# The end of the last block in two halves of two tiles, in a fused attention and LoRA-expert kernel

## The reference

```python
base1 = t @ w1.T
base3 = t @ w3.T
h1 = base1[None] + SCALING * jnp.einsum('etr,efr->etf', jnp.einsum('td,erd->etr', t, a1), b1)
h3 = base3[None] + SCALING * jnp.einsum('etr,efr->etf', jnp.einsum('td,erd->etr', t, a3), b3)
act = jax.nn.silu(h1) * h3
out_e = jnp.einsum('etf,df->etd', act, w2) + SCALING * jnp.einsum('etr,edr->etd', jnp.einsum('etf,erf->etr', act, a2), b2)
out = jnp.einsum('te,etd->td', weights, out_e)
```

## Time and profile before

| | |
|---|---|
| runs | 328.12, 328.14 and 328.87 us, median 328.14 us |
| profiled execution, its own time | 328.73 us |
| its span | 326.9 us (so 1.83 us lie outside the span) |
| mean granted TensorE clock | 0.979 |
| last matmul of `a2_product` ends | 317.50 us |
| last store issued | 324.54 us |

### The profile page before, as it was taken

How to read it: one execution, slowest core, us unless ns; L and a number is a source line. 1 busy time by engine, 2 the same in 40 slices (tenths; PEclk the granted TensorE clock), 3 DMA queues, 4 the chain that set the end, 5 groups by cost and what they waited for, 6 DMA issues and landing times.

```text
span 326.9 us, 4531 instructions
## 1 busy us (share of the span) xinstructions
PE 299.8 (92%) x1520; PEld 241.5 (74%) x1520; DVE 225.1 (69%) x608; ACT 193.9 (59%) x320; POOL 181.7 (56%) x164
## 2 busy tenths in 40 slices
PE   1875779999999999999999999999999999998992
PEld 1654557878888878878787888888787878886771
DVE  3568767697568956696668956795649845963373
ACT  1153566577674786587665777496646756854521
POOL 2111059935886278816794288718781389236910
PEclk9998789999999999999999999999999999999998
DMA  6512001000200002000200011000000000000000
GB/s 179 178 61 65 2 1 64 2 0 1 67 32 0 2 3 94 2 0 3 64 32 3 0 47 52 0 0 2 1 32 2 1 0 34 0 1 3 32 0 32
DMA packets 7127, 8.95 MB, mean 27 GB/s; under 512 B 1216, under 2 KB 3520, under 8 KB 7104
## 3 DMA queue, kind: packets, MB, share of 16 engines
q1 hardware_dynamic: 5520, 7.54, 7.0%
q10 hardware_dynamic: 1584, 1.12, 1.2%
HBM read 6.56 MB, written 2.10 MB: 26 GB/s over the span
## 4 chain that ended last, share of the span: by engine, by line
PE 72%; DVE 9%; issue 6%; POOL 6%; ACT 3%; DMA 2%; SPq 0%; DVEq 0%; POOLq 0%; ACTq 0%
PE h_ps L486 22%; PE h_ps L476 11%; PE z_ps L505 5%; PE b_ps L505 4%; PE odd_ps L519 4%; PE even_ps L344 4%; PE h_ps L456 3%; PE odd_ps L526 2%; PE b_ps L344 2%; PE even_ps L339 2%; PE z_ps L344 2%; PE odd_ps L389 2%; DMA wq_sb<-in_wq_dram 2%; POOL um_lo L1127 1%; PE z_ps L376 1%
## 5 line engine op out<-in xcount | busy, mean ns | idle before, releaser
L699 ACT ACTIVATE silu<-h_ps 128x512 f32<-128x512 f32 x64 | 38.1, 596 | 38.0 <-PE h_ps L486 37.1
L931 DVE TENSOR_TENSOR act_first<-silu,h_ps 128x512 f32<-128x512 f32 x32 | 22.0, 686 | 44.4 <-ACT silu L699 24.4
L486 PE MATMUL h_ps<-um_hi,b_hi 128*128 128x512 f32 x128 | 51.4, 401 | 0.1
L486 PE MATMUL h_ps<-um_hi,b_lo 128*128 128x512 f32 x128 | 50.9, 398 | 0.0
L486 PE MATMUL h_ps<-um_lo,b_hi 128*128 128x512 f32 x128 | 50.8, 397 | 0.0
L1121 POOL TENSOR_TENSOR heads<-e_o,rec_o 128x512 f32<-128x512 f32 x8 | 14.6, 1827 | 62.2 <-DVE rec_o L861 62.2
L1149 POOL TENSOR_TENSOR scaled<-act_second,ratio 128x512 f32<-128x512 f32 x24 | 30.9, 1287 | 21.0 <-DVE act_second L931 20.7
L476 PE MATMUL h_ps<-t_hi,w_hi 128*128 128x512 f32 x64 | 28.3, 442 | 1.9 <-ACT ratio L691 1.9
L1127 POOL TENSOR_TENSOR um_lo<-umf,um_hi 128x1024 fp32r<-128x1024 f32 x8 | 19.1, 2392 | 18.6 <-ACT um_hi L695 18.6
L931 DVE TENSOR_TENSOR act_second<-silu,h_ps 128x512 f32<-128x512 f32 x32 | 21.4, 683 | 10.7 <-PE h_ps L486 10.6
L486 PEld LDWEIGHTS h_ps<-um_lo,b_hi 128*128 128x128 f32 x128 | 24.2, 189 | 5.8
(11 more groups left out here) (161 smaller groups left out, 779.2 us busy)
## 6 DMA issues: line engine op xcount, KB each, us to landing
x_in<-in_x_dram SPq DMA_DIRECT2D x8, 256.0 KB, 3.0
out_dram<-y SPq DMA_DIRECT2D x8, 256.0 KB, 2.0
ctx_in<-in_ctx_t_dram SPq DMA_DIRECT2D x7, 256.0 KB, 3.2
w_raw<-in_w_t_dram SPq DMA_DIRECT2D x2, 256.0 KB, 6.3
b_raw<-in_b_dram ACTq DMA_DIRECT2D x2, 256.0 KB, 4.0
ctx_in<-in_ctx_t_dram ACTq DMA_DIRECT2D x1, 256.0 KB, 3.6
w2a_raw<-in_w_t_dram SPq DMA_DIRECT2D x1, 256.0 KB, 3.7
w2a_raw<-in_a_t_dram SPq DMA_DIRECT2D x1, 256.0 KB, 3.7
```

The costliest lines, as they stand in the source:

```text
L486: mm = nc.tensor.matmul(banks[n % 2][:], b13[w][:, s, cols], um[k][m][:, s, :], start=False, stop=(i == 2), skip_group_check=True)
L699: nc.scalar.activation(silu[:, n % SILU_RING, :], h1_ps[n % 2][:], ACT.Silu).then_inc(silu_done.sem, 1)
L931: nc.vector.tensor_tensor((act_first, act_second)[k][:, c, :], silu[:, n % SILU_RING, :], h3_ps[n % 2][:], ALU.mult).then_inc(act_done.sem, 1)
```

## The change

Only the last block is touched. On DVE the masks' products, the sum `v` and its low part are made in two halves of 256 tokens (two tiles), in the order products and sum of half 0, products and sum of half 1, then the two low parts. ACT makes the two high parts, and later the two copies to `o_t`. PE accumulates half 0 of the output in `odd_ps` and half 1 in `h1_ps[0]`, so that `w2_product` of the last block has six matmuls of 256 columns for a chunk in place of three of 512, and waits for two more semaphores at its first chunk, since `h1_ps[0]` must be free. The three matmuls of the second LoRA product are made for each half, then two transposes for each half, into `even_ps` and `h3_ps[0]`. DVE finishes two tiles and SP stores 128 KB, twice. What is computed stays the same.

```diff
+        last_out, last_turned = (odd_ps, h1_ps[0]), (even_ps, h3_ps[0])
...
-            store(BLOCKS - 1)
-            sp.wait_ge(stored.sem, stored.of(BLOCKS - 1))
+            for i in range(2):
+                sp.wait_ge(last_y, i + 1)
+                sp.dma_start(out[:, LAST * BLK + i * HALF:LAST * BLK + (i + 1) * HALF], flat(y)[:, half(i)])\
+                    .then_inc(last_stored, 16)
+            sp.wait_ge(stored.sem, stored.of(LAST - 1))
+            sp.wait_ge(last_stored, 32)
...
                         pe.wait_ge(o_t_done.sem, o_t_done.of(b - 1))
+                        pe.wait_ge(silu_done.sem, silu_done.of(b))
+                        pe.wait_ge(act_done.sem, act_done.of(b))
...
+                    for h in range(2):
+                        nc.tensor.matmul(last_out[h][:, 0:HALF], w2a2[w][:, c, 0:D], z_split[m][:, c, half(h)],
+                                         start=(c == 0 and i == 0), stop=False, skip_group_check=True)
...
-            b2_product(BLOCKS - 1)
-            tail(BLOCKS - 1)
+            for i in range(2):
+                pe.wait_ge(last_v_hi, i + 1)
+                pe.wait_ge(last_v_lo, i + 1)
+                for j, (w, m) in enumerate(TERMS):
+                    mm = nc.tensor.matmul(last_out[i][:, 0:HALF], b2_split[w][:], v_split[m][:, half(i)], start=False,
+                                          stop=(j == 2), skip_group_check=True)
+                mm.then_inc(last_o_t_mm, 1)
+            pe.wait_ge(y_done.sem, y_done.of(LAST - 1))
+            for i in range(2):
+                pe.wait_ge(last_o_t, i + 1)
+                for t in (2 * i, 2 * i + 1):
+                    mm = nc.tensor.transpose(last_turned[i][:, t * P:(t + 1) * P], o_t[:, t * P:(t + 1) * P], ident[:])
+                mm.then_inc(last_y_mm, 1)
...
-            v_high(BLOCKS - 1)
-            output_t(BLOCKS - 1)
+            for i in range(2):
+                sc.wait_ge(last_v, i + 1)
+                nc.scalar.copy(v_split[0][:, half(i)], v[:, half(i)]).then_inc(last_v_hi, 1)
+            for i in range(2):
+                sc.wait_ge(last_o_t_mm, i + 1)
+                nc.scalar.copy(o_t[:, half(i)], last_out[i][:, 0:HALF]).then_inc(last_o_t, 1)
...
-            v_sum(BLOCKS - 1)
-            v_low(BLOCKS - 1)
-            finish(BLOCKS - 1)
+            ve.wait_ge(a2z_mm.sem, a2z_mm.of(LAST))
+            ve.wait_ge(a2b_mm.sem, a2b_mm.of(LAST))
+            ve.wait_ge(mask_scaled.sem, mask_scaled.of(LAST))
+            ve.wait_ge(v_done.sem, v_done.of(LAST - 1))
+            for i in range(2):
+                for k in range(2):
+                    op = nc.vector.tensor_tensor(v_parts[:, k, half(i)], (z_ps, b_ps)[k][:, half(i)],
+                                                 masks[LAST % 2][:, k, half(i)], ALU.mult)
+                op.then_inc(last_v_part, 1)
+                ve.wait_ge(last_v_part, i + 1)
+                nc.vector.tensor_tensor(v[:, half(i)], v_parts[:, 0, half(i)], v_parts[:, 1, half(i)], ALU.add)\
+                    .then_inc(last_v, 1)
+            for i in range(2):
+                ve.wait_ge(last_v_hi, i + 1)
+                nc.vector.tensor_tensor(v_split[1][:, half(i)], v[:, half(i)], as_f32(v_split[0][:, half(i)]),
+                                        ALU.subtract).then_inc(last_v_lo, 1)
+            ve.wait_ge(w_first_done.sem, w_first_done.of(LAST))
+            ve.wait_ge(stored.sem, stored.of(LAST - 1))
+            for i in range(2):
+                ve.wait_ge(last_y_mm, i + 1)
+                for t in (2 * i, 2 * i + 1):
+                    op = nc.vector.scalar_tensor_tensor(out=y[:, t, :], in0=last_turned[i][:, t * P:(t + 1) * P],
+                                                        scalar=w_first[LAST % 2][:, t:t + 1],
+                                                        in1=x1[LAST % 3][:, t, :], op0=ALU.mult, op1=ALU.add)
+                op.then_inc(last_y, 1)
```

More of the change, by code:

```diff
@@ L275, in build_program @@
         stored = signal("stored", 16)
+        last_v_part = sem("last_v_part")
+        last_v = sem("last_v")
+        last_v_hi = sem("last_v_hi")
+        last_v_lo = sem("last_v_lo")
+        last_o_t_mm = sem("last_o_t_mm")
+        last_o_t = sem("last_o_t")
+        last_y_mm = sem("last_y_mm")
+        last_y = sem("last_y")
+        last_stored = sem("last_stored")
         def tile4(ap):
@@ L287, in build_program, with half @@
         PARTS = (slice(0, 2), slice(2, 3), slice(3, 4))
+        LAST = BLOCKS - 1
+        HALF = BLK // 2
+        def half(i):
+            return slice(i * HALF, (i + 1) * HALF)
         QKV_W_IN, ATTN_W_IN, LORA_W_IN, HIDDEN_W_IN, DOWN_W_IN = 4 * 16, 3 * 16, 5 * 16, 4 * 16, 3 * 16
@@ L517, in w2_product @@
                         pe.wait_ge(o_t_done.sem, o_t_done.of(b - 1))
+                        pe.wait_ge(silu_done.sem, silu_done.of(b))
+                        pe.wait_ge(act_done.sem, act_done.of(b))
                 for i, (w, m) in enumerate(TERMS):
-                    nc.tensor.matmul(out_bank[:], w2a2[w][:, c, 0:D], z_split[m][:, c, :], start=(c == 0 and i == 0),
-                                     stop=False, skip_group_check=True)
+                    if b < LAST:
+                        nc.tensor.matmul(out_bank[:], w2a2[w][:, c, 0:D], z_split[m][:, c, :],
+                                         start=(c == 0 and i == 0), stop=False, skip_group_check=True)
+                        continue
+                    for h in range(2):
+                        nc.tensor.matmul(last_out[h][:, 0:HALF], w2a2[w][:, c, 0:D], z_split[m][:, c, half(h)],
+                                         start=(c == 0 and i == 0), stop=False, skip_group_check=True)
             def b2_product(b):
@@ L966, in v_part @@
                     .then_inc(v_part_done.sem, 1)
[L968 to L975, removed]
             def finish(b):
@@ L1085, in _ @@
                     first_weight(b + 1)
-                v_part(b, 0)
-                v_part(b, 1)
-            v_sum(BLOCKS - 1)
-            v_low(BLOCKS - 1)
-            finish(BLOCKS - 1)
+                if late:
+                    v_part(b, 0)
+                    v_part(b, 1)
+            ve.wait_ge(a2z_mm.sem, a2z_mm.of(LAST))
[23 more added lines that the diff above has]
+                op.then_inc(last_y, 1)
         @block.gpsimd
```

## The result

The changed kernel took 326.59 us (median of 6 runs, 325.95 to 327.58) and the kernel before 328.58 us (median of 6 runs). The ratio is 0.9944, with a 95% interval of 0.993 to 0.9957, so it is faster by 1.84 us (1.4 to 2.3). At 0.56% this lies clear of the 0.3% that can be told here.

What follows compares the result with a forecast made beforehand. Behind the last `a2_product`, a chain of single links over the engines was taken as the bound. Issuing the last store 1.56 us earlier plus 0.28 from its transfer gave 1.84: 328.14 - 1.84 = 326.3 us, range 325.8 to 327.2.

Steps and rivals of the forecast that it cites:

- the issue: Start of the last store on SP, counted from the last `a2_product`'s end: 5.5 us in place of 7.04, 1.56 earlier.
- the store: Last store's transfer: half the bytes in 1 KB packets take 0.42 in place of 0.70 us, 0.28 saved.
- Prices: Assumed 256-column costs: DVE 0.41 us at steps of 0.32, ACT cast 0.42, PSUM copy 0.38, matmuls 0.12 apart.
- Vector part: DVE and ACT, products to low parts in halves: last low part ends at 320.70 in place of 320.92, gaining 0.22.
- PE and ACT: Second LoRA product, copies and transposes in overlapping halves: half 1 done at 321.45, 321.86 and 322.31, gain then 1.04.
- `finish`: DVE's finishing instructions: two take 0.61 us; half 1 starts at 322.34, ends 322.95, last store issued at 322.98.
- added waits: Extra semaphore waits, on DVE's first product and ahead of finishing: taken as costing nothing, at most 0.1 us.
- `w2_product`: Last block on PE: 24 half-width matmuls for 12; 0.05 us more for chunks 0 and 1, covered by idle time.
- small instructions at 0.1 more each: Rival: seven 256-column DVE instructions on the path cost 0.1 more each, losing 0.7: 327.0 us; chance 0.12.
- Stores in series: Rival: second last store is served only after the first lands: 327.7 us, no change to be told; chance 0.07.
- Weight loads at 0.19 a matmul: Rival: 256-column PE matmuls cost 0.19 in place of 0.12, putting 0.41 on the path: 326.7 us; chance 0.07.
- The clock falling ahead of 313.9: Rival: altered `w2_product` tail brings TensorE's fall to 1.2 GHz before the last `a2_product`: 329.6 us, slower; chance 0.03.

Runs made afterwards that it cites:

- second set of runs: The changed kernel run again without any edit, against the kernel before: ratio 0.9954 (0.9936 to 0.9972), tail 7.89 us.
- e7: The kernel before with only the vector part halved, PE waiting for both halves: ratio 0.9995 to the kernel before, tail 9.82 us.
- e2: The changed kernel with the vector part (products, sum, high and low parts) whole again at 512 columns: ratio 0.9965 to the kernel before.
- e5: The changed kernel with already satisfied waits moved ahead of the second LoRA product and the low parts: ratio 0.9937 to the kernel before.
- e1: The changed kernel with one 256 KB last store in place of two of 128 KB: ratio 0.9945 to the kernel before, tail 8.12 us.
- e4: The kernel before with only the last store halved, into two of 128 KB: ratio 1.0 (0.999 to 1.0009), tail 9.74 us.
- e8: The kernel before with eight unused 512-column matmuls keeping PE busy behind the last `w2_product`: ratio 1.0 (0.9986 to 1.0014), tail 9.44 us.
- c2_before: The kernel before, unedited, profiled a third time: tail 9.74 us, last store issued 7.32 us behind the last `a2_product`.
- c1_before: The kernel before, unedited, profiled once more: tail 9.39 us, last store issued 7.03 us behind the last `a2_product`.
- e9: The changed kernel with six unused matmuls keeping PE busy behind the last `w2_product`: ratio 0.9967 to the kernel before, tail 7.91 us.

## Why the prediction was right

The forecast was 326.3 us, a gain of 1.84. The measured gain by the ratio is 1.84 (1.4 to 2.3), and 1.51 in the second set of runs. By the profiles, which leave the start out, it is 1.45 to 1.51, and 1.52 in ns. The mechanism held in each step. Two terms were put 0.32 us too high in all: the issue came 1.34 earlier in place of 1.56, and the store gave 0.18 in place of 0.28. That the first ratio's middle reads 1.84, the forecast to the hundredth, is luck.

- *Prices.* DVE's 256 columns: forecast 0.41, measured 0.41 to 0.43, from PSUM too. Steps 0.33 to 0.34 in place of 0.32. ACT's cast 0.41 and copy 0.37 (0.42 and 0.38). The Trainium skill's formula in "VectorE: DVE Perf Modes" (section on the TRN2 errata) gives 424 ns, and the rows agree with it at least as well as with the one row that I used. Its advice to stay at 512 elements or more did not hold for this chain. A half does cost 0.6 of a whole (0.41 and 0.69 us), and yet the vector part in halves ends 0.15 earlier even by itself (e7), and the last issue comes 0.72 earlier by it where the rest is halved too (e2).
- *Vector part.* Half 1's low part was to end 3.20 behind `a2_product` (320.70 - 317.50) and ended at 3.28.
- *PE and ACT.* Half 1's products were to end at 3.95, the copy at 4.36, the transposes at 4.81. They ended at 4.01, 4.42 and 4.92.
- *`finish`, the term that was mis-sized.* Half 1's finishing was forecast at 4.84, with 0.05 to spare behind half 0's, and started at 5.07. Half 0's came late, as its transposes started 0.15 behind their copy and its finishing 0.55 behind these. I had priced added waits at nothing, with 0.1 as the most. I had looked at DVE's first product, whose blocking wait stands first, and at the gap of 0.03 ahead of the old `finish`, where it does too, and carried that over to an edit that writes it last. e5 takes the satisfied waits away and wins 0.11 at the issue. The rest of the 0.22 by which the issue missed its 5.48 is the 0.08 of the vector part and small change.
- *The store.* 0.28 forecast, as 0.42 in place of 0.70 us of transfer. The transfers took 0.52 and 0.83: the 0.70 came from the fullest quarter and was too short for the whole. In ns the last store lands 1.76 us behind its issue in place of 2.01, 0.25 less. Of that 0.06 are lost again, as the span ends 0.45 behind the landing in place of 0.39. It does so in e1 and e4 too, where SP waits for two counts at the end, and not in e7 and e8, where it waits for one; no run changed that alone. From issue to the end of the span it is 2.21 in place of 2.40.
- *`w2_product`.* At no cost, as forecast.

The rivals: small instructions at 0.1 more each are refuted (0.41 to 0.43). Stores in series are refuted, as their bytes follow each other without a pause. Weight loads at 0.19 a matmul are refuted, as half-width matmuls start 0.12 apart. The clock falling ahead of 313.9 did not happen. But a milder form of it is real, and on the other side than I had it. It fell between 4.1 and 6.3 us behind `a2_product` in the profiles without filling, and it is the old end, with its transposes up to 5.85, that it can meet, more than the new one, whose last transposes end at 4.92. It cost the unchanged kernel 0.29 us in one of three profiles (c2_before), and 0.46 in two kernels that keep its transposes (e4, e7). In none of the profiles of the changed kernel and its kin did it fall ahead of the last transpose. Whether it makes up the distance between the 1.52 of the tails and the 1.84 of the first ratio was not shown (e8).

## What to carry to other kernels

At the end of a kernel a chain of single links over four engines gains from being cut in two even if each half instruction costs 0.6 of a whole one. Work out both halves' start on each engine, as the gain lies in the overlap and not in the shorter instructions: halving the vector part alone took 0.15 off that part, and the same edit was worth 0.72 with the halved rest behind it. Where an instruction waits for several semaphores, write first the wait that will block, as the gaps under e5 suggest. Before cutting finer, ask which input of the first link comes first; using the earlier one beside the last matmuls was worth 0.65 us here, half as much as the whole change. Judge such an edit by the distance from a fixed point of the chain, if the kernel's start varies by more than the edit is worth.

## What the runs showed of the hardware

- Where the wait that blocks is written behind a satisfied one, it is an instruction of its own (51 ns on PE) and the work starts 0.15 us behind its release on PE and 0.14 on DVE (after). Where it is written first or is the only one, the gaps are 0.06 and 0.03 to 0.04 (before, e5).
- The granted clock of TensorE fell at the end at a moment that differs from one execution to the next, in the same kernel too: near 323.7 in the first profile, in the middle of the transposes in c2_before, and between 324.00 and 324.50 in c1_before. With PE filled by matmuls that nothing reads it fell later than in any other profile (e8, e9). Four transposes of 128 columns take 0.66 us at 2.4 GHz and 1.12 at 1.2 GHz.
- A store of 128 KB in packets of 1 KB moved at about 250 GB/s (0.52 us) and one of 256 KB in packets of 2 KB at 312 (0.84 us). The second store's bytes followed the first's at once, and it landed 1.76 us behind its own issue (after).
- Up to the first ratio copy the start took 36.8 to 38.4 us in one and the same code, and everything from there to the last copy 250.42 to 250.53 us. The three starts above 38 are those in which two early matmuls took 1.65 us or more in place of 1.02 to 1.34.
